# Graph layers on one core: VectorE makes a slot's count keys first and the next block's one-hots last, and bounds are read once

## The reference

```python
h = relu(layernorm(x))
for l in range(2):
    weights = softmax(z @ envW[l] + envb[l])             # 4 experts for each node
    agg = segment_sum(z[src], dst) / max(count, 1)       # mean over a node's edges
    out = einsum('nd,kdo->nko', concat([agg, z]), W[l]) + z[:, None, :]
    z = relu(einsum('nk,nko->no', weights, out))
return x + z
```

## Time and profile before

| | us |
|---|---|
| time, median of 3 runs | 2223.12 (2215.25 to 2225.83) |
| the profiled execution's own time | 2221.49 |
| its span | 2219.7 |
| PE busy, share of the span | 1816.4, 82% |
| VectorE busy | 955.2, 43% |
| GpSimd busy | 1395.9, 63% |
| ScalarE busy | 293.0, 13% |
| mean granted clock of TensorE | 0.935 |

### The profile page before, as it was taken

The page is one execution under the profiler, slowest core; times in us unless marked ns, Lnnn a source line. Parts: engine busy times, 40 slices in busy tenths (PEclk is TensorE's granted clock), DMA queues, the critical chain, the costliest instruction groups (busy, mean ns, idle before and its releaser), DMA issues. The chain is left out here.

```text
span 2219.7 us, 41824 instructions
## 1 busy us (share of the span) xinstructions
PE 1816.4 (82%) x10188; PEld 1163.7 (52%) x10189; DVE 955.2 (43%) x2623; ACT 293.0 (13%) x728; POOL 1395.9 (63%) x1451
## 2 busy tenths in 40 slices
PE   0178879887897798979888489998989999889998
PEld 0055546454564454636455256565656565566655
DVE  6565454544544545444453232424343434333332
ACT  7211111110111111111111000000000000000000
POOL 4677664755646557566661476776767676767671
PEclk9889989999998998989999589999999999999999
DMA  7556554554545545555455665666666666666662
GB/s 228 194 162 200 154 145 142 163 176 121 145 149 159 160 119 156 156 145 177 132 160 198 226 172 162 198 179 191 177 193 179 189 178 193 180 182 184 190 177 86
DMA packets 166680, 376.12 MB, mean 169 GB/s; under 512 B 40733, under 2 KB 96598, under 8 KB 164182
## 3 DMA queue, kind: packets, MB, share of 16 engines
q0 software_dynamic: 90112, 276.91, 44.0%
q10 hardware_dynamic: 41592, 67.44, 8.7%
q1 hardware_dynamic: 34654, 27.46, 4.0%
HBM read 326.03 MB, written 44.94 MB: 167 GB/s over the span
## 5 line engine op out<-in xcount | busy, mean ns | idle before, releaser
L668 POOL DMA_INDIRECT ring<-zp_dram,gather_idx x1376 | 1324.0, 962 | 722.9 <-POOLq L88 361.0
L1197 PE MATMUL mix_ps<-w_sb,turned 128*128 128x512 f32 x1568 | 775.6, 636 | 21.8 <-issue 21.4
L1120 PE MATMUL agg_ps<-ring,onehot 128*128 x3440 | 629.6, 284 | 8.5 <-issue 8.5
L1114 PE MATMUL agg_ps<-ring,onehot 128*128 x1720 | 487.0, 283 | 135.8 <-PEq L88 104.7
L1197 PEld LDWEIGHTS mix_ps<-w_sb,turned 128*128 128x128 f32 x1568 | 299.4, 202 | 343.0 <-issue 340.1
L1120 PEld LDWEIGHTS agg_ps<-ring,onehot 128*128 128x128 bf16 x3440 | 341.5, 99 | 102.8 <-issue 33.2
L834 DVE SCALAR_TENSOR_TENSOR mix<-mix_ps,wts,mix 128x256 f32<-128x256 f32 x392 | 189.7, 484 | 416.8 <-DVEq L88 388.0
L724 DVE TENSOR_TENSOR onehot<-nodes,dst_t 128x512 bf16<-128x512 f32 x430 | 270.6, 695 | 117.0 <-issue 117.0
L1114 PEld LDWEIGHTS agg_ps<-ring,onehot 128*128 128x128 bf16 x1720 | 172.5, 100 | 213.7 <-issue 183.5
L1147 PE MATMUL agg_ps<-zp,counts_sb 128*128 128x256 bf16 x1568 | 261.0, 273 | 0.0
L1144 PE MATMUL agg_ps<-zp,counts_sb 128*128 128x257 bf16 x784 | 213.5, 272 | 4.1 <-PEq L88 4.1
(11 more groups left out here) (134 smaller groups left out, 806.0 us busy)
## 6 DMA issues: line engine op xcount, KB each, us to landing
ring<-zp_dram,gather_idx POOLq DMA_INDIRECT x1376, 3.3
counts_sb<-a_dram ACTq DMA_DIRECT2D x9, 1568.0 KB, 10.3
a_dram<-counts_sb ACTq DMA_DIRECT2D x8, 1568.0 KB, 6.6
zp_dram<-zp SPq DMA_DIRECT2D x7, 1344.0 KB, 5.7
zp_dram<-parts ACTq DMA_DIRECT2D x49, 192.0 KB
zp<-zp_dram SPq DMA_DIRECT2D x5, 1344.0 KB, 13.9
z_dram<-z_out ACTq DMA_DIRECT2D x49, 128.0 KB
z_in<-z_dram ACTq DMA_DIRECT2D x49, 128.0 KB
```

Of the source, the lines that this page charges most:

```text
L668: pool.indirect_dma_start(out=ring[:, k, t, 0:3 * D], out_offset=None, in_=zp_dram[l], in_offset=bass.IndirectOffsetOnAxis(ap=gather_idx[: ...
L1114: mm = pe.matmul(agg_ps[:, bank, 0:D + 1], onehot[:, h, place, t, :], rows[:, :, 2 * D:3 * D + 1], start=place == 0 and t == 0, stop=True, ...
L1120: mm = pe.matmul(agg_ps[:, bank, 0:D], onehot[:, h, place, t, :], rows[:, :, part * D:(part + 1) * D], start=False, stop=True, skip_group_ ...
L1197: mm = pe.matmul(mix_ps[i][:, :], turned[:, what, c, :], w[:, i * HALF:(i + 1) * HALF], start=n == 0, stop=n == 3)
```

## The change

On DVE, in a slot of layer 0 that builds windows, the four windows' bounds are read once and kept, and their first keys are made before everything else. Then the bounds of the block after next are read, then comes `split`, and the one-hots follow it. `other_keys` uses the bounds that were kept. `s_mixfree` is raised by ACT when it has taken `s_over`, no longer by DVE in `split`. On PE, one number for each group of four windows (the longest window, computed once with the table) is read; a window's own length is read only if that number is over 2. The conditions for units beyond the fourth are nested on PE and DVE.

```diff
@@ make_plan
+                        settle(nc.vector.tensor_reduce(most, win_n.rearrange("o (g j) -> o g j", j=GROUP), AX.X,
+                                                       ALU.max))
+                        nc.vector.tensor_copy(plan[:, WX:WX + WINS // GROUP], most)
@@ more_units
-            def more_units(eng, n, use):
-                for i in range(STRAIGHT, PLACES):
-                    with eng.If(n > i):
-                        use(i)
+            def more_units(eng, n, use, others=lambda: None):
+                with eng.If(n > STRAIGHT):
+                    use(STRAIGHT)
+                    with eng.If(n > STRAIGHT + 1):
+                        use(STRAIGHT + 1)
+                        others()
@@ vector
-                    def compare_block(blk, h):
-
+                    def bounds(blk):
+                        lo, hi = units_of(dve, blk)
+                        return blk, lo, hi, dve.snap(hi - lo)
+
+                    def compare_block(head, h):
+
+                        blk, lo, hi, n = head
                         settle(nc.vector.tensor_scalar(nodes[:, h, :], node0[:], block_base[:, bass.ds(blk, 1)], None,
                                                        ALU.add))
-                        lo, hi = units_of(dve, blk)
-                        n = dve.snap(hi - lo)
...
-                    def other_keys(dn, g, j):
-                        w, lo, hi = window_tiles(dn, g, j)
+                    def other_keys(tiles, j):
+                        w, lo, hi = tiles
...
                     def split():
                         take(dve, s_hi)
-                        dve.sem_inc(s_mixfree, 1)
...
                             for k in range(ORDER):
+                                build = first and k < NG
                                 if k != PER_ROUND - 1:
                                     compare_rest((k + 1) % 2 if k < PER_ROUND else 0)
+                                tiles = []
+                                if build:
+                                    for j in range(GROUP):
+                                        tiles.append(window_tiles(dn, k, j))
+                                        tile_keys(tiles[j][0], j, tiles[j][1])
+                                head = None
                                 if k < PER_ROUND - 2:
-                                    compare_block(sparse_block(dve, r, k + 2), k % 2)
+                                    head = bounds(sparse_block(dve, r, k + 2))
                                 elif k == PER_ROUND - 1:
-                                    compare_block(sparse_block(dve, r, PER_ROUND), 0)
+                                    head = bounds(sparse_block(dve, r, PER_ROUND))
+                                if first and k:
+                                    split()
+                                if head:
+                                    compare_block(head, k % 2 if k < PER_ROUND - 2 else 0)
...
-                                build = first and k < NG
-                                if first and k:
-                                    split()
-                                if build:
-                                    for j in range(GROUP):
-                                        first_keys(dn, k, j)
                                 take_mean((k + 1) % 2)
...
                                 if build:
                                     for j in range(GROUP):
-                                        other_keys(dn, k, j)
+                                        other_keys(tiles[j], j)
                                 combine(l)
@@ scalar
                     def begin(l):
                         if l < L - 1:
                             take(act, s_over)
+                            act.sem_inc(s_mixfree, 1)
@@ tensor
+                    def most_tiles(dn, g):
+                        return pe.value_load(plan[0:1, bass.ds(pe.snap(dn * NG + (g + WX)), 1)], min_val=1,
+                                             max_val=TILES)
...
-                        with pe.If(n > 2):
-                            with pe.Fori(2, n, 2) as _:
-                                trip(False)
+                        with pe.If(most > 2):
+                            n = window_tiles(dn, g, j)
+                            with pe.If(n > 2):
+                                with pe.Fori(2, n, 2) as _:
+                                    trip(False)
...
-                        next_at = {0: 0, 1: 1, 3: 2, 4: 3}
...
                                 if build and place in window_at:
-                                    summed = window(window_at[place], tiles)
-                                if build and place in next_at:
-                                    tiles = window_tiles(*build, next_at[place])
+                                    summed = window(*build, window_at[place], most)
+                                if build and place == 0:
+                                    most = most_tiles(*build)
```

More of the change, by code:

```diff
@@ L69, in gnn_kernel @@
     BP, WP, WN, DM = 0, NB + 1, NB + 1 + WINS, NB + 1 + 2 * WINS
-    RR = DM + R_ALL + 2
+    WX = DM + R_ALL + 2
+    RR = WX + WINS // GROUP
     TT = RR + 1
@@ L253, in gnn_kernel @@
             win_n = mix[0:1, 0:WINS]
+            most = mix[0:1, WINS:WINS + WINS // GROUP]
             ints = ed("ints", [1, 2, WINS], I32)
@@ L625, in gnn_kernel @@
             STRAIGHT, PLACES = 4, 6
+            assert PLACES == STRAIGHT + 2
             def head_units(eng, n, use, between):
@@ L862, in _ @@
                             keep_z(0, 0)
-                        compare_block(0, 0)
+                        compare_block(bounds(0), 0)
                         compare_rest(0)
-                        compare_block(1, 1)
+                        compare_block(bounds(1), 1)
                         if first:
@@ L912, in _ @@
                                                          skip_runtime_bounds_check_because="the last blocks by edge")
-                                compare_block(blk, 0)
+                                compare_block(bounds(blk), 0)
                                 if first:
@@ L1130, in sparse_sum, with others @@
                         head_units(pe, head["n"], add_unit, between)
-                        more_units(pe, head["n"], add_unit)
-                        with pe.If(head["n"] > PLACES):
-                            with pe.Fori(head["lo"] + PLACES, head["hi"]) as u:
-                                add(pe.snap(unit_no(u) % RU), PLACES)
+                        def others():
+                            with pe.If(head["n"] > PLACES):
+                                with pe.Fori(head["lo"] + PLACES, head["hi"]) as u:
+                                    add(pe.snap(unit_no(u) % RU), PLACES)
+                        more_units(pe, head["n"], add_unit, others)
                     def dense_sum(l, bank, between):
@@ L1157, in window_tiles, with window @@
                         return pe.value_load(plan[0:1, bass.ds(w + WN, 1)], min_val=1, max_val=TILES)
-                    def window(j, n):
+                    def most_tiles(dn, g):
+                        return pe.value_load(plan[0:1, bass.ds(pe.snap(dn * NG + (g + WX)), 1)], min_val=1,
+                                             max_val=TILES)
+                    def window(dn, g, j, most):
                         p = j % 2
@@ L1187, in tail @@
                         pe.wait_ge(s_w[l], 16 * CC)
-                        steps, summed, tiles = list(steps), None, None
+                        steps, summed, most = list(steps), None, None
                         window_at = {1: 0, 3: 1, 4: 2, 5: 3}
-                        next_at = {0: 0, 1: 1, 3: 2, 4: 3}
                         step_at = {2: 1, 6: 3} if build else {0: 1, 2: 1, 4: 1, 6: 1}
```

5 lines of the change are left out of this document (1 added, 4 removed).

## The result

The changed kernel takes 2186.62 us, the median of 4 runs (2185.06 to 2189.22); beside it the kernel before takes 2221.4 us (4 runs, 2215.25 to 2225.83). The ratio is 0.985, with a 95% interval of 0.982 to 0.988. The forecast was 2193: 28 us less were expected of this median, and 35 came.

The account below looks back on a forecast made before the run. It took layer 0 to be bound by VectorE's late maximum holding up TensorE's third window. Layer 0 -26.5 and nesting -4 made -30.5: 2221.5 to 2191, plus 1.6 for the median, 2193; own range 2173 to 2211, overall 2160 to 2230.

Parts of the forecast that it names:

- What sets a slot: Layer 0, slot 1: the logits' maximum, late in VectorE's queue, holds up the third window; the slot takes 23.0 us.
- the measured ring: Slot 1 of layer 0, 23.0 us: combine, maximum, ScalarE's move, third and fourth window, second half of `mix_ps`, combine.
- Slots 1 and 2, -8 us: Layer 0, ten slots without further trips: sum 0.3 us earlier by keys first, 0.4 by TensorE's reads; -0.8 each.
- my own mark: Sign set beforehand: the prediction is wrong if the maximum in slot 1 moves by over 1 us.
- Slot 0, +6 us: Layer 0, four slots without further trips: maximum 2.0 us later, clock +1.2, products -1.3, TensorE's reads -0.4; +1.5 each.
- Products: VectorE's products in layer 0: kept bounds make them ready 3.4 us earlier, 0.85 a window; combine gains 1.3 where late.
- Slot 3, -3 us: Layer 0, no one-hots: maximum about 1.2 us earlier, combine 1.3; two of four slots gain 1.4.
- Further trips, -21.5 us: Layer 0, windows needing more keys: -0.6 in three slots 0 and 1, -10.4 in four, -10.5 in three slots 3.
- The first round, 0: Layer 0, four window slots of the first round: paced by the gather, so left out of the costing.
- Nested conditions, -4 us: Five-unit blocks: one skipped test of 0.27 us goes about once in a round and layer; bounds 0 and -10.
- the Trainium skill's rule of jumps: Taken branches beyond what is prefetched stall the engine; on some 60 of 82 sparse sums +230 us, chance 0.02.
- Clock: TensorE's low clock after waits costs 1.2 us, always in slot 0, in two thirds of slots 1 and 2.

Follow-up runs that it names:

- the second trace of the changed kernel: The changed kernel run again without a further edit, on a chip where the kernel before takes 2221.12 us: 2190.3 us, ratio 0.988.

## Why the prediction was right, step by step

*What sets a slot.* Right, and shown: with 3 us more ahead of the maximum, slots 1 and 2 grow by 3.8 and 3.0 us each over the second trace of the changed kernel; with 3.7 us less in slot 1 it shrinks by 3.2 in the round shown. By the measured ring one must look at the maximum, not at the keys.

*Slots 1 and 2, -8 us.* Right in sum, wrong in its make-up. The ten plain slots gave -8.5 (-5.4 in the second trace of the changed kernel). But I forecast the maximum 0.3 us earlier in both; it came 1.2 us earlier in slot 1 (medians 14.5 and 13.3) and 0.3 in slot 2 (14.4 and 14.1). By my own mark, more than 1 us in slot 1, that step failed: the sum that balanced two reads against two pauses was mis-sized. The rows of slot 1 show where. The block's read behind the keys, put at 0.5 us, leaves 0.1 us between the last key and `split`. The keys of four windows, which I had left as they were, take 5.4 us where they took 6.0. The first window's read stands open for 0.86 us, not 0.6. The slots themselves made it even: three plain slots 1 gave -5.3, seven slots 2 only -3.2.

*Slot 0, +6 us.* The sum was right, +6.3 over four plain slots (+7.2 in the second trace). The maximum came later by 1.2 us, not 2.0 (medians 17.5 and 18.7), so its term was 0.8 too high; the low clock behind TensorE's wait of 4 to 7.6 us did come, as forecast. In the run with the old order back in slot 0, that slot is 9.0 us shorter over seven rounds, which fits; the run had slot 1's edit beside it.

*Products.* I had 0.85 us for each window's second read, 3.4 in all. The wait ahead of the products fell from 4.3 to 1.3 us, so 3.0, or 0.76 a window.

*Slot 3, -3 us:* -3.0.

*Further trips, -21.5 us.* Seven such slots 0 and 1 gave -6.0 in the first trace of the changed kernel and -11.2 in the second, where I had -11; three in slot 3 gave -9.4 and -10.0, where I had -10.5. So one trace doesn't size this term to better than 5 us. But a step in it was wrong. For a third or fourth window I had taken away the whole wait, because its keys "will be there when TensorE asks". They can't be: a window's second keys go to the place of its first ones (`s_bfree`), so VectorE makes them only when TensorE has multiplied the first pair. The fourth window of slot 0 in the last round, changed kernel, TensorE and VectorE:

```profile
1079.24 0.86 PE L1186 MATMUL win_ps<-build_key,build_lo 128*128 128x392 bf16 x2
1081.51 0.81 PE L1186 MATMUL win_ps<-build_key,build_lo 128*128 128x392 bf16 x2 [1.40 <-PEq L89]
```

```profile
1080.36 0.25 DVE L780 TENSOR_SCALAR build_lo<-lo,lo_t 128x128 bf16<-128x128 f16 x1 [3.89 <-DVEq L89]
```

VectorE stood for 3.89 us with its weights done and began 0.26 us behind the first pair. In the four such slots 0 and 1 the wait of the further trip was 1.82, 4.37, 2.34 and 2.42 us; it is 1.40, 2.04, 1.40 and 1.40 now, and in the second trace within 0.03 of that. Beside it the wait for the third window's PSUM place, which is the maximum's, didn't go: it was 0.3 to 2.7 us in these slots and is 2.1 to 5.4.

*The first round, 0.* Its first `lg_ps` comes 2.4 us later (139.8 from 137.4) and the second round 2.1 us earlier (258.5 from 260.6). I had left it to the gather; what paid there I did not try to find.

*Nested conditions, -4 us.* The places I named are right, the gap ahead of `lg_ps` is 0.27 us at five units now. Slots 4 and 5 gave -3.1 and -2.9 over seven rounds, where I had -2 for both together, and layer 1 gave 3 to 6 (five traces of 993 to 996 against one of 999.1), where I had 2. The run of nesting alone gave 5 us of 2929 with an interval that holds zero, and its layer 1 took 1332.5 us where the two runs with bounds kept, whose layer 1 is the old one, took 1329.2 and 1330.4. So the size is read from the slots and not shown by itself. It has a rival that I didn't test: VectorE now reads a block's bounds ahead of `nodes`, in layer 1 too, and the pause behind `nodes` fell by 0.7 us. The stall that the Trainium skill's rule of jumps ("Runtime: NRT & Kernel Launch", "Instruction fetch mechanics") would have brought did not show with nesting: slots 4 and 5, which have little else changed, did not grow, and with nesting alone, on a chip where TensorE stood without a cause, the ratio was 0.998. Whether these jumps leave what had been prefetched, no run shows.

*Clock.* I said a granted clock falling in layer 0 would prove me wrong. It went from 0.93 to 0.95 in layer 0 (90 us to the last round). By slot, over seven rounds, it went from 0.90 to 0.85 in slot 0, from 0.87 to 0.88 in slot 1, from 0.95 to 0.97 in slot 2 and from 0.98 to 1.00 in slot 3. That the low clock would follow more of TensorE's waits holds for slot 0 alone.

*In all:* layer 0 -28.7 against -28.5 with its half of the branches; layer 1 -6.0 against -2. So the total is in part luck. In the first trace two errors cancel inside layer 0: further trips gave 6.1 us less than I said, slots 4 and 5 and the first round 6.1 more. In the second (-30.8 and -3.1) further trips came out as forecast, and plain slots 1 and 2 fell 2.6 us short instead. The terms that were undersized in both are those that I put down to nesting, -4 forecast against some -10 to -12 in slots 4 and 5 and layer 1.

*What stays open.* How the 29 us of layer 0 divide between the order, VectorE's kept reads and TensorE's single read on a chip like the first: the single parts never ran on one. On the other two, kept reads gave 0.4 to 0.8%, the order alone 0 to -0.5%, and all three 1.3%. Part of the order's gain may need the reads gone, since the order puts the first window's read ahead of the first key; that is argued, not shown.

## What to carry to other kernels

Find the one result whose lateness sets the ring, here a 4-column maximum queued behind some 9 us of keys and one-hots, and move what the ring doesn't need behind it: the change reordered what stood ahead of the maximum and gained 1.2 to 1.5%, putting 4 us of it behind the maximum in one slot of six, with the old order back in the slot that had lost, gained another 1.3%. Choose the order slot by slot, for the same change was worth -1.8 us in a plain slot 1 and +1.6 in a plain slot 0 (-1.4 and +1.8 in the second trace). A delay of known length put into each suspected place told more about this ring than taking the parts of the change apart. And before forecasting that a wait goes, ask what its releaser waits for: the further keys could not come earlier than their place was free.

## What the runs showed of the hardware

The kernel before took 2221 us in two measurements and 2929 and 2932 us on two other chips. There, with bounds kept, TensorE's mean granted clock was 0.82 and 570 to 580 us of its idle time (561 and 570 gaps in two runs) had no cause in the profile, where the changed kernel on the first chip has 7. VectorE's longest pause on the way to the maximum was 2.9 to 5.8 us in slots 1 and 2. The two instruction queues moved nearly the same on both kinds (203 or 204 packets, 3.3 MB, and 111 to 119 packets). What differs there isn't known.

The slot 1 shown without a wait ran all its window matmuls at 0.49 us a pair; behind a wait of 2.67 us a pair took 0.81. And 3 us of delay in 16 slots went with 48 us of later maxima and 9 us more of TensorE's busy time.
